# An attention stage that keeps other tiles of probabilities whole: tiles 10 and 18 in place of 7, 17 and 18

## The reference, cut to what matters

```python
qkv = x @ W_qkv.T                                    # x: layernorm of the input, 2048 x 512
attn = einsum('bhqd,bhkd->bhqk', q, k) * SCALE       # 16 heads of width 32
attn = where(causal, attn, -inf)
out = einsum('bhqk,bhkd->bhqd', softmax(attn), v)
x = x + layernorm(out.reshape(b, s, d) @ W_proj.T)
```

## Time and profile before

| | us |
|---|---|
| median of three executions | 1714.2 |
| the profiled execution | 1712.4 |
| its span in the trace | 1710.6 |
| PE busy | 1655.9 (97%) |
| DVE, ACT, POOL busy | 1157.1, 1104.7, 889.2 |
| one head inside the loop | 40.26 |

### The profile page before, as it was taken

The page is one execution under the profiler, slowest core; times in us unless marked ns, Lnnn a source line. Parts: engine busy times, 40 slices in busy tenths (PEclk is TensorE's granted clock), DMA queues, the critical chain, the costliest instruction groups (busy, mean ns, idle before and its releaser), DMA issues.

```text
span 1710.6 us, 30467 instructions
## 1 busy us (share of the span) xinstructions
PE 1655.9 (97%) x9262; PEld 1369.2 (80%) x9262; DVE 1157.1 (68%) x2377; ACT 1104.7 (65%) x1684; POOL 889.2 (52%) x764
## 2 busy tenths in 40 slices
PE   8999999999999999999986999999999999999996
PEld 7987777777777777776765999999999999999992
DVE  6437777777777777777797666566665566556545
ACT  3212888888788888786686666566565565556544
POOL 2321777777777777772763343343343343433423
PEclk9999999999999999999997999999999999999998
DMA  8676211111111111122654888887887787788776
GB/s 254 187 223 197 52 51 50 49 50 49 49 49 49 49 49 50 49 67 84 243 201 163 272 256 244 240 273 218 260 239 216 225 261 214 209 244 237 196 191 215
DMA packets 103715, 276.87 MB, mean 162 GB/s; under 512 B 19833, under 2 KB 37625, under 8 KB 93625
## 3 DMA queue, kind: packets, MB, share of 16 engines
q1 hardware_dynamic: 78169, 213.29, 37.9%
q0 software_dynamic: 25440, 62.27, 16.9%
HBM read 194.75 MB, written 63.72 MB: 151 GB/s over the span
## 4 chain that ended last, share of the span: by engine, by line
PE 87%; DVE 5%; DMA 3%; ACT 2%; issue 2%; POOL 1%; SPq 0%; DVEq 0%; ACTq 0%; POOLq 0%
PE p_prj L91 25%; PE a_op L883 12%; PE a_sp L901 8%; PE a_mp L842 7%; PE p_at_ps L91 7%; PE p_logit_ps L91 6%; PE e_qp L91 5%; PE a_op L874 5%; PE p_ht_ps L2057 3%; PE e_vp L91 3%; PE p_at_ps L2080 2%; DVE part_max L759 1%; PE a_mp L845 1%; PE a_sp L905 1%; PE a_shared L860 1%
## 5 line engine op out<-in xcount | busy, mean ns | idle before, releaser
L709 POOL TENSOR_TENSOR prob_lo<-prob,prob_hi 128x1024 fp32r<-128x1024 f32 (+1 forms) x211 | 450.6, 2158 | 162.4 <-DVE prob_hi L788 157.5
L759 DVE TENSOR_REDUCE part_max<-a_mp 128x1 f32<-128x512 f32 (+2 forms) x600 | 357.8, 610 | 83.3 <-PE a_mp L842 61.8
L1446 POOL DMA_INDIRECT acc_rows<-m_y_out,m_row_ids x108 | 176.1, 1630 | 411.9 <-ACT m_y_out L1615 391.9
L744 ACT ACTIVATE prob<-a_sp 128x1024 f32<-128x1024 f32 x320 | 293.3, 930 | 64.6 <-PE a_sp L901 32.6
L91 PE MATMUL p_prj<-m_w_hi,m_ht_hi 128*128 128x352 f32 x888 | 297.3, 335 | 1.6 <-DVE m_ht_lo L1855 1.4
L91 PE MATMUL p_prj<-m_w_lo,m_ht_hi 128*128 128x352 f32 x888 | 288.1, 324 | 0.0
L91 PE MATMUL p_prj<-m_w_hi,m_ht_lo 128*128 128x352 f32 x888 | 287.4, 324 | 0.0
L1879 DVE TENSOR_TENSOR m_w_lo<-m_w_raw,m_w_hi 128x704 fp32r<-128x704 f32 (+1 forms) x357 | 270.9, 798 | 23.2 <-ACT m_w_hi L1621 22.8
L1621 ACT ACTIVATE m_w_hi<-m_w_raw 128x704 fp32r<-128x704 f32 (+1 forms) x357 | 229.0, 714 | 19.1 <-PE p_prj L91 16.8
L1865 DVE TENSOR_TENSOR m_at_lo<-p_at_ps,m_at_hi 128x384 fp32r<-128x384 f32 x111 | 61.8, 557 | 252.5 <-ACT m_at_hi L1607 252.5
L731 ACT ACTIVATE prob_hi<-prob 128x1024 fp32r<-128x1024 f32 x216 | 203.3, 941 | 6.9
(11 more groups left out here) (314 smaller groups left out, 3311.5 us busy)
## 6 DMA issues: line engine op xcount, KB each, us to landing
m_w_raw<-wexp SPq DMA_DIRECT2D x51, 1408.0 KB, 6.7
m_w_raw<-wexp SPq DMA_DIRECT2D x51, 768.0 KB, 6.5
qk_parts<-rows SPq DMA_DIRECT2D x64, 256.0 KB, 3.2
multi<-qk_parts SPq DMA_DIRECT2D x42, 256.0 KB, 5.1
acc_rows<-p_zeros SPq DMA_DIRECT2D x2, 4352.0 KB, 18.5
v_head<-v_all SPq DMA_DIRECT2D x16, 520.0 KB, 3.0
k_stack<-qk_parts SPq DMA_DIRECT2D x21, 256.0 KB, 3.9
q_stack<-qk_parts SPq DMA_DIRECT2D x21, 256.0 KB, 6.1
```

What stands on the lines that cost most here:

```text
L709: nc.gpsimd.tensor_tensor(prob_lo[:, t % RING, :, c0:NB], prob[:, t % RING, :, c0:NB], f32(prob_hi[:, t % RING, :, c0:NB]), ALU.subtract). ...
L744: nc.scalar.activation(prob[:, t % RING, :, c0:NB], sp_[:, t % 2, :, c0:NB], ACT.Exp, scale=SCALE).then_inc(prob_ready, 1)
L759: nc.vector.reduce_max(part_max[:, qb, kb:kb + 1], mp[:, n % 2, 0:width], AX_X).then_inc(piece_done, 1)
L1446: nc.gpsimd.indirect_dma_start(acc_dram[sum_of(t)], bass.IndirectOffsetOnAxis(ap=row_id(t), axis=0), y_out[:, t % 4, :], None, compute_op= ...
```

## The change: which tiles are whole, and where one piece stands

- `WHOLE` becomes {10, 18}. It was {7, 17, 18}. So in heads 0 to 14, tiles 7 and 17 are split and multiplied in parts, and tile 10 is multiplied whole. Head 15 keeps {7, 17, 18}, as `WHOLE_LAST`, which the new function `whole_tiles` chooses.
- `HI_DVE` loses tile 9, so ACT makes its high part. With the new `WHOLE`, ACT also makes the high parts of 7 and 17, and no longer that of 10.
- `LO_POOL` is all tiles but 0, 1, 2 and the whole ones, so POOL makes the low parts of 7 and 17, and no longer that of 10.
- `PIECES_AT` has 2 in place of 3 in step 14, and 3 in place of 2 in step 17. Pieces 27, 30 and 33 each come one step later. Head 0 has its own table, which stays.

```diff
-PIECES_AT = (0, 0, 0, 0, 0, 3, 3, 3, 3, 3, 2, 3, 2, 3, 3, 3, 3, 2, 2, 2)
+PIECES_AT = (0, 0, 0, 0, 0, 3, 3, 3, 3, 3, 2, 3, 2, 3, 2, 3, 3, 3, 2, 2)
...
-WHOLE = {7, 17, 18}
-HI_DVE, HI_DVE_LAST = {2, 3, 9}, {1, 2, 3, 4, 5, 8, 9, 11, 13, 15, 19}
+WHOLE, WHOLE_LAST = {10, 18}, {7, 17, 18}
+HI_DVE, HI_DVE_LAST = {2, 3}, {1, 2, 3, 4, 5, 8, 9, 11, 13, 15, 19}
...
+def whole_tiles(h):
+    return WHOLE_LAST if isinstance(h, int) and h == H - 1 else WHOLE
...
-            eng.wait_ge(hi_act, h * (NS - len(HI_DVE | WHOLE)) + (t - count_before(tiles | WHOLE, t) + 1))
+            eng.wait_ge(hi_act, h * (NS - len(HI_DVE | WHOLE)) + (t - count_before(tiles | whole_tiles(h), t) + 1))
...
-            if t not in hi_dve_tiles(h) | WHOLE:
+            if t not in hi_dve_tiles(h) | whole_tiles(h):
...
-            if t in lo_pool_tiles(h) | WHOLE:
+            if t in lo_pool_tiles(h) | whole_tiles(h):
...
-            if t in WHOLE:
+            if t in whole_tiles(h):
```

More of the change, by code:

```diff
@@ L639, in wait_lo @@
         else:
-            eng.wait_ge(lo_dve, h * (NS - len(LO_POOL | WHOLE)) + (t - count_before(tiles | WHOLE, t) + 1))
+            eng.wait_ge(lo_dve, h * (NS - len(LO_POOL | WHOLE)) + (t - count_before(tiles | whole_tiles(h), t) + 1))
     def sync_part(sp):
```

## The result

The changed kernel took 1699.51, 1696.42, 1699.64 and 1700.35 us, a median of 1699.58, beside 1713.88 for the kernel before (four executions each). The ratio is 0.9912, with a 95% interval of 0.9900 to 0.9924. The forecast was 1697, with a range of 1692 to 1704. The profiled execution took 1699.51 us, 12.9 less than the profiled one of before; its span is 1697.8.

What follows compares the result with a forecast made beforehand. PE's list of matmuls was taken to bound each head (39.89 busy of 40.26 us). Products -13.2, piece -3.5 and head 0's wait -0.2 sum to -16.9: 1695.5 from the profiled 1712.4, so 1697 by the median, range 1692 to 1704.

Steps and rivals of the forecast that it cites:

- PE's products: Heads 0 to 14: tiles 7 and 17 split save 0.78 each, tile 10 whole costs 0.68; -0.88 a head, -13.2 us.
- The piece: Step 15: piece 30's 0.34 us wait for DVE goes; 0.25 a head over 14 heads, -3.5 us.
- The upper bound of 0.45: Most the moved piece could gain a head in step 15: the 0.34 wait and part of the weight load behind it.
- the walk of its queue: POOL's parts timed in the new order against PE's wants: margins 1.9, 1.5, 2.4 and 1.4 us, no cost.
- 1.4 + 1.1 us a head: POOL's low part of tile 17: lateness decides once the margin of 1.4 and the 1.13 gained per head are spent.
- ACT: Three high parts more, one less: 32.6 to 34.7 busy of 39.1 a head, costing nothing.
- case B: ACT becomes a bound from tile 12 on: two places at 0.25 to 0.5, 15 times, +7.5 to 15, 1704 to 1710; 9%.
- Gives nothing: DVE losing the cast of tile 9, which stands beside PE's work, was said to gain nothing.
- A: The wait for DVE in step 15 only moves, as DVE has the same reductions: 1700.5 us; 17%.
- C: POOL is late with tile 17's low part, PE waits 1.8 a head: +10, 1724 us; 4%.
- E: PE is held by something else in the same steps, shorter tiles only turn into waits: 1714 us; 3%.
- D: More gained: all 0.45 of step 15 and some smaller DVE waits, 14 x 0.3 more, 1693 us; 9%.

## Why the prediction was right, and where it was not

- **PE's products**, -0.88 a head: each row came as read (0.78 for tile 7, 1.51 for tile 10). Alone, the edit gave 0.8 a head and 10.5 us in the stage, of the 13.2 in the sum. 1.5 of the missing 2.7 are the waits for loads.
- **The piece**, -3.5: the wait in step 15 goes and does not come back in step 16. The size was low: 0.31 a head over the looped heads and 4.3 us in the stage. The upper bound of 0.45 was the nearer end.
- **POOL**: the walk of its queue was right to 0.2 us at tile 17, and the experiment with one subtraction more confirmed the limit, which the prediction put at 1.4 + 1.1 us a head.
- **ACT**: no cost, as said. The waits of PE and of its weights for ACT in the looped heads have hardly changed: two matmuls and 17 weight loads before, four matmuls and 13 weight loads now, each by 0.15 to 0.24 us. The far end of case B was added up wrongly: 1697 and 15 are 1712, not 1710, and the range does not rest on it.
- **DVE's cast of tile 9** was weighed wrongly. "Gives nothing" is true of a cast beside an idle POOL, as in the row read. In the changed order POOL is never idle there, and the same cast costs 24 us in the stage. The change moved it to ACT, so the sum did not suffer, but that was luck: the reason given for that part of the change was missed. It is what lets POOL's longer list stand at all. The rule of the Trainium skill was looked up for the low parts only, and not for the cast. The prediction also says that no row of before shows such an overlap. That holds of the rows it picked, but the trace of before has one, in head 15, where a cast of 512 numbers took 2.27 in place of the 0.42 of the same form at 779.79:

```profile
770.73 2.36 POOL L709 TENSOR_TENSOR prob_lo<-prob,prob_hi 128x1024 fp32r<-128x1024 f32 x1 [1.72 <-ACT prob_hi L731]
```

```profile
771.11 2.27 DVE L788 CAST prob_hi<-prob 128x512 fp32r<-128x512 f32 x1 [2.78 <-ACT prob L744]
```

- **The missing step** is the load. The sum treated everything from the head's last scores to step 5 as PE's own time, and what else runs against it was not asked. It cost 1.9 of the 16.9 us.
- So the stage came to 14.7 of 16.9: 1.9 lost to the loads, 0.8 more from the piece, and the rest in the products, which gave 0.8 a head and not 0.88. The medians differ by 14.3 and the two profiled executions by 12.9, since the parts ahead of the stage and behind it move by up to 4 us from one execution to the next. Of the cases, the forecast's own mechanism held; A, B, C and E did not occur, and part of D did.

## What to carry to other kernels

When PE is the bound and the others have room in sum, walk each queue in order with the trace's pitches, and compare every deadline: here this gave the limit of POOL to a fraction of a microsecond, in a kernel that had not been run. When a stretch gets shorter, list what else was hidden in it, transfers too: they keep their length. The price of a cast, or of a subtraction with both inputs in SBUF, read on DVE beside an idle POOL holds only as long as POOL stays idle there. And before a few microseconds between two traces are put down to an edit, compare the granted clock of the same stretch in both: here one stretch of 3.4 us made two edits seem to give more apart than together.

## What the runs showed of the hardware

- A DVE cast of 128x1024 from SBUF to SBUF takes 0.69 us beside an idle POOL, and up to 2.49 beside POOL's subtractions, ending 0.56 after one of them. A pair of DVE subtractions of 1024 and 512 numbers takes 1.84 alone and 4.40 beside them, where the first ends 1.09 after POOL's last. Cast and subtraction alike end 0.13 less than their own time (0.69 and 1.22) after POOL's. DVE's reductions from PSUM keep their mean of 0.69 (512 numbers) in both kernels.
- The same six transfers of 256 KB in every head land after a median of 3.9 to 6.1 us each, by the list of transfers of the changed kernel; the three that PE waited longest for took 6.9, 7.1 and 8.1. The spread is as large as the slack to which such a kernel is tuned.
- Waits of 1.4 to 2.2 us in a PE that is otherwise busy were followed by 3.4 or 6.8 us at 1.2 GHz in six of the thirteen looped heads of the kernel with the later loads, and not in the other seven, whose waits were 1.3 to 2.1. In that kernel the clock cost half as much as the waits themselves, 12 us beside 22.
